# A vision tower of four layers on one core: patches split for fp32r, a second attention opened group by group, and image sums among the turns

## The reference

```python
out = jnp.einsum('bsk,ek->bse', patches, w) + b          # patches: k = 3*16*16 = 768, e = 128
...
route_prob = jax.nn.softmax(xt.astype(jnp.float32) @ Wr + br, axis=-1)   # layer 1: one of 8 experts
...
out = out * (p_max / jax.lax.stop_gradient(p_max))[:, None]
...
scores = jnp.einsum('bhts,bhus->bhtu', Q, V) / jnp.sqrt(jnp.float32(S))  # layer 2: 8 heads of 64
...
W = jax.nn.softmax(scores, axis=-1)
C = jnp.einsum('bhtu,bhus->bhts', W, V)
...
routing_input = x.mean(axis=1)                                           # layer 3: a router for each image
logits = jax.nn.relu(routing_input @ r_w1 + r_b1) @ r_w2 + r_b2
```

## Time and profile before

| | us |
|---|---|
| runs before | 1223.40, 1224.66, 1228.81 |
| median | 1224.66 |
| the profiled execution | 1230.08 |
| its span | 1228.3 |

### The profile page before, as it was taken

The page is one execution under the profiler, slowest core; times in us unless marked ns, Lnnn a source line. Parts: engine busy times, 40 slices in busy tenths (PEclk is TensorE's granted clock), DMA queues, the critical chain, the costliest instruction groups (busy, mean ns, idle before and its releaser), DMA issues. The chain is left out here.

```text
span 1228.3 us, 29277 instructions
## 1 busy us (share of the span) xinstructions
PE 1099.0 (89%) x8508; PEld 911.7 (74%) x8508; DVE 907.4 (74%) x2770; ACT 845.2 (69%) x2822; POOL 529.2 (43%) x885
## 2 busy tenths in 40 slices
PE   8899989999998999887397699998899899869996
PEld 5678868888887788786387577786678688657884
DVE  0488868999975889855665488786899788754774
ACT  1498878888885555456243478887878499846995
POOL 0379983545204278855352543323432011033552
PEclk9999979999999999988599689999999999958998
DMA  7300002321210000001622200000434100023441
GB/s 294 96 2 2 3 1 79 103 71 63 62 40 23 1 2 1 2 1 41 200 59 49 63 11 2 10 2 1 123 115 111 29 2 2 2 80 115 129 130 47
DMA packets 50824, 66.68 MB, mean 54 GB/s; under 512 B 8100, under 2 KB 30904, under 8 KB 50552
## 3 DMA queue, kind: packets, MB, share of 16 engines
q1 hardware_dynamic: 44552, 53.39, 14.4%
q0 software_dynamic: 4432, 6.59, 2.1%
q10 hardware_dynamic: 1696, 4.98, 1.0%
HBM read 58.32 MB, written 6.71 MB: 53 GB/s over the span
## 5 line engine op out<-in xcount | busy, mean ns | idle before, releaser
L495 DVE TENSOR_TENSOR f_parts<-T,f_parts 128x512 fp32r<-128x512 f32 (+1 forms) x240 | 186.2, 814 | 23.8 <-ACT f_parts L479 22.4
L471 ACT ACTIVATE T<-quad_bank,f_b1s 128x512 f32<-128x512 f32 (+1 forms) x240 | 150.5, 646 | 49.8 <-PE quad_bank L442 42.5
L442 PE MATMUL quad_bank<-XP,f_wp 128*128 128x512 f32 (+1 forms) x720 | 166.8, 376 | 0.2 <-ACT T L471 0.2
L442 PEld LDWEIGHTS quad_bank<-XP,f_wp 128*128 128x128 f32 x720 | 126.5, 190 | 25.3 <-issue 0.9
L479 ACT ACTIVATE f_parts<-T 128x512 fp32r<-128x512 f32 (+1 forms) x240 | 132.2, 591 | 0.0
L965 ACT ACTIVATE a_late<-quad_bank,a_shift 108x108 f32<-108x108 f32 x352 | 119.0, 363 | 2.5 <-DVE a_shift L1051 2.3
L455 PE MATMUL bank<-f_parts,f_wp 128*128 128x512 f32 (+1 forms) x480 | 114.6, 374 | 4.7 <-DVE XT L504 2.0
L455 PEld LDWEIGHTS bank<-f_parts,f_wp 128*128 128x128 f32 x480 | 84.3, 189 | 22.9 <-DVE a_late L524 2.7
L384 POOL TENSOR_TENSOR f_wp<-f_ws,const 128x512 fp32r<-128x512 f32 (+1 forms) x32 | 33.2, 1038 | 123.1 <-DMA f_ws<-in_f_w 63.9
L965 ACT ACTIVATION_READ_ACCUMULATOR a_late<-quad_bank,a_shift 108x1 f32 x352 | 77.8, 221 | 0.0
L771 POOL TENSOR_TENSOR a_ve<-a_mv,const 108x1 f32<-108x1 f32 x44 | 8.3, 189 | 153.0 <-DVE a_mv L1108 153.0
(11 more groups left out here) (478 smaller groups left out, 3109.9 us busy)
## 6 DMA issues: line engine op xcount, KB each, us to landing
a_late<-f_gates SPq DMA_DIRECT2D x64, 256.0 KB, 3.2
a_wqk<-in_a_wqk SPq DMA_DIRECT2D x24, 256.0 KB, 2.5
f_ws<-in_f_w SPq DMA_DIRECT2D x16, 256.0 KB, 3.8
pats<-in_patches SPq DMA_DIRECT2D x5, 648.0 KB, 10.6
pats<-in_patches ACTq DMA_DIRECT2D x5, 648.0 KB, 14.7
a_late<-f_gates SPq DMA_DIRECT2D x16, 128.0 KB, 3.5
f_w1a<-in_f_w SPq DMA_DIRECT2D x1, 2048.0 KB, 11.1
f_w2a<-in_f_w SPq DMA_DIRECT2D x1, 2048.0 KB, 15.9
```

The lines of the kernel that those rows point to most:

```text
L442: mm = pe.matmul(self.m.quad_bank[:, q % 4, 0:w], self.wp[0][:, e % 2, a, c * 128:(c + 1) * 128], self.xp[:, b, t0:t0 + w], start=((a, b) ...
L471: act.activation(self.full[:, q % 4, 0:w], self.m.quad_bank[:, q % 4, 0:w], self.func, bias=self.b1s[:, e * self.chunks + c:e * self.chunk ...
L495: dve.tensor_tensor(self.lo[:, q % self.ring, 0:w], self.full[:, q % 4, 0:w], self.hi[:, q % self.ring, 0:w], ALU.subtract).then_inc(self. ...
```

## The change

- Patches: chunks 1 to 5 are projected in three fp32r products instead of one in fp32. ScalarE makes the high part of `tokw` and of each half chunk, VectorE the low part; two buffers of parts alternate, so the high part of chunk n waits until chunk n-2 is projected. Chunk 0 stays fp32. ScalarE takes its biases and VectorE its copies two chunks behind.
- Experts: `gates()` runs in two pieces in turns 18 and 20 of VectorE's loop.
- Second attention: VectorE takes each group by itself (sum, `bn_stats`, `bn_aggr`), adds EPS for the variance itself and computes the offsets itself; GpSimd keeps only the power (`root`). The chunks 0 to 2 arrive ahead of step 0, interleaved with the copies; the later groups come in pairs in steps 0 to 4, behind `mix.stats` and ahead of `odd`. Half of chunk 0 is normalised by VectorE. GpSimd fetches 6 to 9 and 10 to 12 between the powers.
- Routing: `image_sums(n)` stands between the turns from the fourth on, three chunks behind.

```diff
             def project(n):
                 c, k = CHUNKS[n]
-                pe.wait_ge(first_half[n], 16)
                 at_least(pe, biased, n - 1)
...
+                        pe.wait_ge(w_split, 1)
+                        pe.wait_ge(p_split, 2 * (n - 1) + i + 1)
...
+                            for w, x in PARTS:
+                                mm = pe.matmul(m.bank[n % 2][:, 0:k * P], wparts[:, w, kc * D:(kc + 1) * D], parts[:, n % 2, x, kc, 0:k * P],
...
+            def high(n):
+                k = CHUNKS[n][1]
+                at_least(act, proj_psum, n - 1)
+                for i, (first, end) in enumerate(halves):
+                    act.wait_ge((first_half, second_half)[i][n], 16)
+                    act.activation(parts[:, n % 2, 0, first:end, 0:k * P], pats[:, n, first:end, 0:k * P], ACT.Copy).then_inc(p_high, 1)
...
+            act.activation(wparts[:, 0, :], tokw[:, :], ACT.Copy).then_inc(w_high, 1)
+            high(1)
+            high(2)
+            act.wait_ge(b_loaded, 16)
+            biases(0)
+            for n in range(3, len(CHUNKS)):
+                high(n)
+                biases(n - 2)
...
+            low(1)
+            low(2)
+            rows_out(0)
+            for n in range(3, len(CHUNKS)):
+                low(n)
+                rows_out(n - 2)
...
             arriving.all_stored(pool)
             arriving.fetch(pool, range(0, 6))
-            scale_shift(0)
-            arriving.fetch(pool, range(6, 8))
-            scale_shift(1)
-            arriving.fetch(pool, range(8, 12))
-            scale_shift(2)
+            root(0)
+            arriving.fetch(pool, range(6, 10))
+            root(1)
+            arriving.fetch(pool, range(10, 13))
+            root(2)
             normalise(8)
-            arriving.fetch(pool, range(12, 14))
+            arriving.fetch(pool, range(13, 14))
             for t in range(last):
+                if 1 <= t <= len(ARRIVALS) - 3:
+                    root(2 + t)
                 if t + 9 < G:
                     normalise(t + 9)
                 arriving.fetch(pool, range(14 + 2 * t, min(16 + 2 * t, G)))
-                if t in (2, 4, 6):
-                    scale_shift(2 + t // 2)
...
-            def statistics(s):
...
+            def arrive(g):
+                arriving.add(dve, g)
+                dve.wait_ge(arriving.added, g + 1)
+                dve.bn_stats(x_bn[:, g, :], m.H[:, g * D:(g + 1) * D]).then_inc(x_bn_ready, 1)
+                dve.wait_ge(x_bn_ready, g + 1)
+                dve.bn_aggr(x_mv[:, g, :], x_bn[:, g, :]).then_inc(x_mv_ready, 1)
...
-            for s in range(2):
-                statistics(s)
+            for g in range(4):
+                arrive(g)
+            variance(0)
+            arrive(4)
+            offsets(0)
+            chunk_norm(range(2, 4))
+            arrive(5)
             chunk_low(0)
+            arrive(6)
+            arrive(7)
+            variance(1)
             odd(0, 1)
+            offsets(1)
             odd(0, 3)
+            arrive(8)
+            arrive(9)
             chunk_low(1)
+            arrive(10)
+            arrive(11)
+            variance(2)
             odd(0, 5)
             odd(0, 7)
-            statistics(2)
+            offsets(2)
...
+                if 1 <= t <= len(ARRIVALS) - 3:
+                    offsets(2 + t)
...
-                if t in (1, 3, 5):
-                    statistics(3 + t // 2)
...
                     mix.stats(dve, g)
+                if 3 + t < len(ARRIVALS):
+                    c, k = ARRIVALS[3 + t]
+                    for g in range(c, c + k):
+                        arrive(g)
+                    variance(3 + t)
                 if t // 4 + 1 < nb:
                     odd(t // 4 + 1, 2 * (t % 4) + 1)
...
+ARRIVALS = CHUNKS[:3] + [(c, 2) for c in range(3 * QUAD, G, 2)]
...
+                if j == 18:
+                    gates()
+                if j == 20:
+                    scaled_gates()
             output(tiles - 1)
-            gates()
...
+            def image_sums(n):
...
                 mm.then_inc(turned, 1)
...
+                if n >= 3:
+                    image_sums(n - 3)
+            for n in range(len(CHUNKS) - 3, len(CHUNKS)):
+                mm = image_sums(n)
             mm.then_inc(sums_psum, 1)
```

More of the change, by code:

```diff
@@ L184, in _, with low, rows_out @@
         def _(dve):
-            for n, (c, k) in enumerate(CHUNKS):
+            def low(n):
+                k = CHUNKS[n][1]
+                for i, (first, end) in enumerate(halves):
+                    dve.wait_ge(p_high, 2 * (n - 1) + i + 1)
+                    dve.tensor_tensor(parts[:, n % 2, 1, first:end, 0:k * P], pats[:, n, first:end, 0:k * P],
+                                      parts[:, n % 2, 0, first:end, 0:k * P], ALU.subtract).then_inc(p_split, 1)
+            def rows_out(n):
+                c, k = CHUNKS[n]
                 dve.wait_ge(turned, n + 1)
                 dve.tensor_copy(m.H[:, c * D:(c + k) * D], m.bank[2 + n % 2][0:P, 0:k * D]).then_inc(h_ready, 1)
+            dve.wait_ge(w_high, 1)
+            dve.tensor_tensor(wparts[:, 1, :], tokw[:, :], wparts[:, 0, :], ALU.subtract).then_inc(w_split, 1)
+            low(1)
[4 more added lines that the diff above has]
+                rows_out(n - 2)
+            for n in range(len(CHUNKS) - 2, len(CHUNKS)):
+                rows_out(n)
             dve.wait_ge(h_ready, len(CHUNKS))
@@ L1432, in _ @@
             chunk_high(0)
+            even(0, 0)
             chunk_norm(1)
-            even(0, 0)
             even(0, 2)
@@ L1470, in _, with variance, offsets, chunk_norm @@
         def _(dve):
-            def statistics(s):
-                c, k = CHUNKS[s]
-                arriving.add(dve, s)
-                for g in range(c, c + k):
-                    dve.bn_stats(x_bn[:, g, :], m.H[:, g * D:(g + 1) * D])
-                dve.drain()
-                for g in range(c, c + k):
-                    ins = dve.bn_aggr(x_mv[:, g, :], x_bn[:, g, :])
-                ins.then_inc(x_stats, 1)
+            def arrive(g):
[4 more added lines that the diff above has]
+                dve.bn_aggr(x_mv[:, g, :], x_bn[:, g, :]).then_inc(x_mv_ready, 1)
+            def variance(i):
+                c, k = ARRIVALS[i]
+                dve.wait_ge(x_mv_ready, c + k)
+                dve.tensor_scalar(x_scale[:, c:c + k], x_mv[:, c:c + k, 1:2].rearrange("p g c -> p (g c)"), EPS, None,
+                                  ALU.add).then_inc(x_var, 1)
+            def offsets(i):
+                c, k = ARRIVALS[i]
+                dve.wait_ge(x_rstd, i + 1)
+                dve.scalar_tensor_tensor(out=x_shift[:, c:c + k], in0=x_mv[:, c:c + k, 0:1].rearrange("p g c -> p (g c)"), scalar=-1.0,
+                                         in1=x_scale[:, c:c + k], op0=ALU.mult, op1=ALU.mult).then_inc(x_known, 1)
+            def chunk_norm(groups):
+                dve.wait_ge(x_known, 1)
+                for g in groups:
+                    dve.tensor_scalar(m.XN[:, g * D:(g + 1) * D], m.H[:, g * D:(g + 1) * D], x_scale[:, g:g + 1], x_shift[:, g:g + 1],
+                                      ALU.mult, ALU.add).then_inc(c_normed, 1)
             def chunk_low(s):
@@ L1923, in gates, with scaled_gates @@
                 then(dve.tensor_tensor(pr[:, :, :], pr[:, :, :], wide(tot[:, :]), ALU.mult))
+            def scaled_gates():
+                then = chained(dve, gate_scaled)
                 then(dve.tensor_reduce(result.gate[:, :], pr[:, :, :], AX, ALU.max))
@@ L2718, in _ @@
         def _(pe):
+            def image_sums(n):
+                c, k = CHUNKS[n]
+                if n == 0:
+                    pe.wait_ge(m.rw_loaded, 16)
+                pe.wait_ge(xn_ready, n + 1)
+                for g in range(c, c + k):
+                    mm = pe.matmul(m.quad_bank[:, 0, g * TB:(g + 1) * TB], m.XN[:, g * D:(g + 1) * D], const("member", P), start=True, stop=True)
+                return mm
             keep_busy(pe, m, m.bank[3], 2)
@@ L2725, in _ @@
                 mm.then_inc(turned, 1)
-            pe.wait_ge(m.rw_loaded, 16)
-            for n, (c, k) in enumerate(CHUNKS):
-                pe.wait_ge(xn_ready, n + 1)
-                for g in range(c, c + k):
-                    mm = pe.matmul(m.quad_bank[:, 0, g * TB:(g + 1) * TB], m.XN[:, g * D:(g + 1) * D], const("member", P), start=True, stop=True)
+                if n >= 3:
+                    image_sums(n - 3)
+            for n in range(len(CHUNKS) - 3, len(CHUNKS)):
+                mm = image_sums(n)
             mm.then_inc(sums_psum, 1)
```

78 lines of the change are left out of this document (41 added, 37 removed).

## The result

The changed kernel takes 1216.5 us (median of 13 runs, 1212.7 to 1221.8) beside 1226.1 us (1221.6 to 1229.4) for the kernel before, timed with it: a ratio of 0.993, interval 0.991 to 0.995, or 8.8 us with 6.6 to 11.0. Taken again later (g4_changed_again) it was 0.990 (0.988 to 0.993), 11.9 us. Forecast were 6.4 us and 1218.3: the direction, the range and the biggest part were right, the size too small.

A forecast was written before the change was run, and what follows sets the result against it. TensorE was taken as busy throughout the experts' loop but waiting for others in the second attention's opening. Terms -2.9 + 0.7 - 4.4 + 0.2 = -6.4 us, off the 1224.7 median, gave 1218.3 us; range 1211 to 1224.5.

The forecast's parts named there:

- patches: Patch projections: 18 fp32r matmuls a chunk at 0.20 us save 0.73 us in each of four chunks, -2.9 us.
- experts' gates: Experts' loop and its end: stalls of 1.6 us less 0.9 us freed at the end, +0.7 us.
- opening: Opening of the second attention: -3.9 us up to group 1's masked sums and -0.5 in steps 1 to 5, -4.4.
- routing: Routing stage: TensorE, with image sums spread among the turns, ends at 1094.3 against 1094.1, +0.2 us.
- The bound of +1.0: Patches' worst case: VectorE at 874 ns for 512 elements makes each chunk 0.2 us slower than before.
- The stall: Experts' loop: gates in turns 18 and 20 stall TensorE about 1.0 and 0.6 us, 1.6 in all.
- the end: Behind the experts' loop: the last row store, then the fetch 1.0 us later, so 0.8 to 0.9 us freed, not 1.94.
- this gain doesn't reach the scores: Second attention's opening: the first projection comes near 682 instead of 684.83, but VectorE's 9 us queue keeps scores near 693.6.
- Rival A: Second attention's opening: TensorE's clock stays up without the stand, 2 to 3 us more gain, 1215.5 us; chance 0.17.
- B (8.3): Second attention's opening: arrivals not covered, steps 1 to 4 take 8.3 us each, opening -1.0, 1221.7 us; chance 0.23.
- C (9.43): Second attention: VectorE's queue holds TensorE in steps 1 to 4 as in the 9.43 us step; 1226.4 us; chance 0.08.
- the upper bound: Routing's worst case, +0.8 us: XN of chunk 4, pushed back by the late turn, comes last.

The follow-up runs named there:

- f4_arrivals_late: The changed kernel with the arrivals of groups 8 to 11 moved back behind the last odd copy of the first projections; ratio 0.996 (0.994 to 0.998).
- g3_scalar_norms: The changed kernel with all four normalisations of chunk 0 on ScalarE again; ratio 0.992 (0.990 to 0.995).
- e4_routing: The kernel before with only the image sums spread among the turns; ratio 1.001 (0.999 to 1.003).
- g1_fours: The changed kernel with late arrivals in blocks of four (four and two) in steps 1, 3 and 5 instead of pairs; ratio 0.994 (0.992 to 0.996).
- the four g runs: Changed kernel with late arrivals in fours, pairs ahead of the divisions, chunk 0's normalisations on ScalarE, and unchanged; ratios 0.994, 0.994, 0.992, 0.990.
- e and f runs: Four kernels adding one part each to the kernel before (0.998, 1.002, 0.996, 1.001); four variants built on the changed kernel (0.992, 0.993, 0.992, 0.996).

## Why the prediction was right, and where it was short

| part | forecast | traces, means of like profiles | that part alone, timed |
|---|---|---|---|
| patches | -2.9 | -4.0 | -2.4 (-5.5 to +0.9) |
| experts' gates | +0.7 | -0.1 (one profile against five) | +2.0 (-0.7 to +4.6) |
| opening | -4.4 | -6.9 | -5.2 (-8.1 to -2.4) |
| routing | +0.2 | +0.4 | +1.0 (-1.9 to +3.8) |
| sum | -6.4 | -10.6 | the whole: -8.8 and -11.9 |

The parts alone add to -4.6 us with an uncertainty of about 6, each having some 3 of its own: that doesn't speak against the whole, and doesn't show that they add up either. The traces are the finer measure.

**Patches.** Right in kind. The cadence is 3.98 us, for which the working had 4.1 (3.6 + 0.43 rounded up, with 4.36 taken for the twelve): a full step saves 0.81 us, not 0.73. The half chunk, counted at nothing, saves 0.1 (2.08 us from its start to its turn against 2.19). In this profile the steps from chunk 0 on saved 0.3, 0.5 and three times 0.8 us, where I had four of 0.73, and with the half chunk and a first matmul 0.2 us earlier that is the 3.6 us of this pair of profiles; the mean's 4.0 has the spread of the old ones in it. The bound of +1.0, VectorE at 874 ns for 512 elements, was never near: 1.51 us for 1296.

**Gates.** The stall was sized well (1.6 forecast, 1.7 measured by one profile, stands of 1.34 and 0.98 us seen). The step that failed is the end: I took the start of the fetch 1.0 us behind its release from the earlier trace rows and put it behind the store's landing too. But it runs from the start of the phase, beside the store's way to its landing: the fetch starts 1.5 us after the store's issue ends (659.61 - 658.12) instead of 2.99 (668.39 - 665.40). So 1.8 us are gained and not 0.9.

**Opening, ahead of group 1.** Forecast -3.9, mean of six against four profiles -5.6 (27.2 against 32.7). The wait for group 8 did go, and f4_arrivals_late brings it back. The step that failed is "this gain doesn't reach the scores": group 0's scores start 19.5 us behind the first sum instead of 21.4 (means of six and four), and those 1.9 us cover the 1.7 that the forecast lacked; from the scores to group 1's masked sum it is 7.7 us instead of 11.4, -3.7 where the forecast had -3.9. g3_scalar_norms shows that the first projection's start reaches the scores. I had queued 9 us of VectorE's work behind it; an arrival takes 0.80 to 0.85 us and not 0.95, and the queue ran inside ScalarE's and TensorE's waits. Rival A's mechanism has a share in it: the first projection takes 4.01 us where the earlier trace rows had 4.69, the granted clock being up some 13 us behind the first sum instead of 18; by means it takes 3.3 us instead of 4.5. How much of that reaches the scores was not separated from the earlier start (10.2 us behind the first sum instead of 13.3).

**Opening, steps.** Forecast -0.5, measured -1.3 (35.0 against 36.3). Steps 2 to 4 take 6.7 to 7.0 us, 0.4 over a plain one, not 1.0: two arrivals with variance and offset are 2.0 us of VectorE, and 1.4 us of the plain step's 6.54 were free there, not the 1.2 of two named waits. Rivals B (8.3) and C (9.43) are out as the kernel stands. Both priced the arrivals by the step of four groups, and that was dear through its block and the clock behind it, as e4_routing and g1_fours show. Moved ahead of the divisions (g2_ahead) the pairs do come to 7.4 to 7.9, near B.

**Routing.** +0.37 for +0.2: the 0.41 us wait for XN of chunk 4 that stood in the upper bound.

**Base.** I took the sum off the median and said that the profile's 5.4 us above it lay in no one place. That was needed: the profiled execution of the changed kernel lies 3.8 us below its median, so the two spans alone would have given 17.4. That 1218.3 came so near to 1216.5 is in part luck: the median that I started from, 1224.7, was 1.5 us below the one timed beside the changed kernel, and hid as much of the gain that the forecast lacked. By the difference, rival A's 9.2 us are nearer to the 8.8 measured than my 6.4. The errors of the parts did not cancel: three of the four came out better than forecast, routing 0.2 us worse.

## What to carry to other kernels

Split a helper engine's block of work into pieces that fit its own idle time in each step: the block costs its length once, and again in its own step or the one after it when TensorE comes back at half its clock (means of such steps: 0.82 and 0.78 granted). Before a wait is priced from a row, ask whether it belongs to what ends (then it goes with it) or to what starts. And where two executions of the same code differ by more than the change, read each stage in every profile that has it unchanged, and compare like with like in the granted clock.

## What the runs showed that I had not expected

- The same stage of the same code has two or three lengths, told apart by one fall of TensorE's clock: the experts' loop 80, 83 or 85 us, the stage behind the opening 99.1 or 100.6 us. In that one the fall lies 70 to 80 us behind its start (0.83 for 10 us against 1.00), and what decides was not found; in the loop it follows the length of one stand, as shown above.
- The third attention, untouched by every kernel here, takes 121.3 to 123.3 us in six profiles (the first pair and the four g runs, chip 6) and 132.3 to 136.2 in the eight of the e and f runs (chips 5 and 12), at the same granted clock of 1.00 in its middle. TensorE has 246 matmuls in 20 us in the first and 222 in the second, waiting 0.30 us for a_h and 0.18 for a_pT in the slower rhythm. The cause is open; it moves the kernel more than the whole change, and only runs beside each other on one chip can be compared.
